# Segment maxima in two levels with an earlier return, and the fourth pass's degree gathers moved to the third pass

## What is computed

```
x += GAT2(GAT1(h))        # two attention layers, 4 heads, self loops
x += sum_e v[src]*s / sum_e s,  s = exp(clip(k[src].q[dst]/sqrt(32)))
x += poincare(h' + attention sum of h'[src])   # one head
x += relu-GCN twice, with norm = w * rsqrt(deg_out[src]*deg_in[dst] + 1e-12)
```

```
e  = leaky_relu(al_s[src] + al_d[dst])
m  = segment_max(e, dst)
ee = exp(e - m[dst]);  s = segment_sum(ee, dst)
out = segment_sum(ee / s[dst] * feat[src], dst)
```

## Time and profile before

| what | value |
| --- | --- |
| median of three runs | 5259.4 us |
| the profiled execution: device time | 5256.77 us |
| its span, first to last instruction | 5255.0 us |
| mean granted TensorE clock | 0.926 of full speed |
| TensorE matmul, busy | 4453.1 us (85%) |
| VectorE, busy | 4208.4 us (80%) |
| ScalarE, busy | 2973.3 us (57%) |
| GpSimd, busy | 3241.2 us (62%) |
| HBM traffic | 209 GB/s mean |

### The profile page before, as it was taken

One profiled execution on the slowest core, in us unless ns is written; L12 is line 12 of the kernel. 1 busy time (PEld: TensorE's weight loads), 2 busy tenths in 40 slices (PEclk: granted clock), 3 DMA queues, 4 the chain that ended last, 5 costly groups with the idle time before them and its releaser, 6 DMA issues. The chain is left out here.

```text
span 5255.0 us, 75793 instructions
## 1 busy us (share of the span) xinstructions
PE 4453.1 (85%) x21191; PEld 3340.7 (64%) x21191; DVE 4208.4 (80%) x12564; ACT 2973.3 (57%) x7552; POOL 3241.2 (62%) x2813
## 2 busy tenths in 40 slices
PE   3999999999958888857888799999956748988887
PEld 2888888888836666635666566666634436765555
DVE  5999999999968888759999478888868878965554
ACT  2999999999914444424444467777745534431111
POOL 3776666666267776447777265555277746647777
PEclk9999999999979999968888899999978878999998
DMA  4888888888734444347777556566457766654443
GB/s 134 300 313 309 311 310 310 308 311 309 287 123 129 128 127 127 95 121 250 256 269 264 174 159 190 184 182 191 157 183 253 254 219 187 204 155 133 151 151 130
DMA packets 645561, 1096.74 MB, mean 209 GB/s; under 512 B 82230, under 2 KB 465654, under 8 KB 645021
## 3 DMA queue, kind: packets, MB, share of 16 engines
q1 hardware_dynamic: 525866, 837.50, 46.5%
q0 software_dynamic: 119168, 253.97, 16.5%
q10 hardware_dynamic: 112, 0.40, 0.0%
HBM read 523.88 MB, written 575.95 MB: 209 GB/s over the span
## 5 line engine op out<-in xcount | busy, mean ns | idle before, releaser
L851 PE MATMUL mm<-w,tt 128*128 128x264 f32 x3136 | 733.6, 387 | 2.6 <-ACT tt L895 2.6
L1399 POOL DMA_INDIRECT got<-F,index x392 | 506.1, 1291 | 281.5 <-PE acc L1557 176.6
L851 PEld LDWEIGHTS mm<-w,tt 128*128 128x128 f32 x3136 | 583.1, 191 | 93.3 <-ACT tt L895 2.8
L1566 ACT ACTIVATE rows<-acc 128x260 f32<-128x260 f32 (+1 forms) x588 | 227.4, 387 | 561.0 <-PE acc L1557 561.0
L1553 PE MATMUL acc<-got,sel 128*128 128x260 f32 (+1 forms) x1176 | 426.1, 449 | 99.6 <-DVE sel L1528 93.2
L817 POOL DMA_INDIRECT place<-PLACE,place_ix x392 | 412.9, 1053 | 119.5 <-issue 119.5
L2698 DVE SCALAR_TENSOR_TENSOR agg<-mask,agg,acc 128x128 f32<-128x128 f32 x784 | 248.0, 344 | 255.7 <-PE acc L2685 141.3
L789 POOL DMA_INDIRECT xd<-in_x_dram,index x196 | 229.5, 1171 | 315.5 <-DMA XD<-xd 284.5
L851 PE MATMUL mm<-wl,tt 128*128 128x264 f32 x1568 | 413.7, 387 | 1.3 <-ACT tt L895 1.3
L1288 PE MATMUL kv<-wkv,ht 128*128 128x512 f32 x784 | 372.7, 598 | 0.1
L1206 POOL DMA_INDIRECT got<-Q,index x196 | 202.0, 1030 | 260.4 <-DVE sc L2284 213.9
(11 more groups left out here) (391 smaller groups left out, 13285.4 us busy)
## 6 DMA issues: line engine op xcount, KB each, us to landing
F<-f1o SPq DMA_DIRECT2D x97, 528.0 KB, 5.9
F<-f2o SPq DMA_DIRECT2D x97, 528.0 KB, 3.2
HL<-ho SPq DMA_DIRECT2D x97, 528.0 KB
xin<-in_x_dram SPq DMA_DIRECT2D x97, 512.0 KB, 5.8
H<-h SPq DMA_DIRECT2D x97, 512.0 KB, 3.4
X<-x3o SPq DMA_DIRECT2D x97, 512.0 KB, 3.4
out_dram<-oo SPq DMA_DIRECT2D x97, 512.0 KB
drow<-DSTF SPq DMA_DIRECT2D x84, 448.0 KB
```

Source lines behind the costliest of these rows:

```text
L851: last = nc.tensor.matmul(mm[PAIR[stage, q]][:, r, 0:F2W], lhs[:, q, 2 * r + k, :], w[:, k, :], start=(k == 0), stop=(k == KB - 1))
L1399: nc.gpsimd.indirect_dma_start(out=buf[:, n % SLOTS, t, :], out_offset=None, in_=table, in_offset=bass.IndirectOffsetOnAxis(ap=index[:, n ...
L1566: nc.scalar.activation(self.rows[:, n % 2, t, :], self.acc[tile % 2][:, 0:self.width], ACT.Copy)\
```

## The change

The maxima are found in two levels. `turn_scores` makes one transpose: head and tile together (28 rows, or 7) become partitions, the 128 edges of a tile the free dimension. `segment_most` scans the 128 edges forward and back, for all tiles at once (`near`), then multiplies the first and last column with an identity (`edges`). `turn_back` makes two matmuls with a matrix of ones, which put each tile's first and last maximum on all partitions (`ends`), and one transpose of `near`. `differences` runs two scans of 8 numbers per head over the tiles of the group (with tables `across_tiles` that say where a target spans a whole tile), adds a penalty where an edge's target is not the neighbouring tile's (`beyond`), and takes the maximum of the three. What is carried to the next group is written by ScalarE behind the exponentials. The tables are made once, at the head of the first pass. `penalties` issues two DMAs per head (8, or 2), each of 7 rows of 128 numbers, in place of one. The turn back stands behind tile 2 in the first and second pass and behind tile 1 in the fourth. The 84 degree gathers of the fourth pass are issued in the third pass, two behind the gathers of each of the first 42 groups.

```
             def turn_scores(self, pe, n):
                 hold(pe, self.done["top"], n + 1, None)
                 hold(pe, self.done["most"], n, None)
-                for t in range(GS):
-                    last = nc.tensor.transpose(self.turned[0:self.h, t * P:(t + 1) * P], self.top[:, t, :], ident[:, :])
-                last.then_inc(self.done["turned"], 1)
+                nc.tensor.transpose(self.turned[0:self.h * GS, 0:P], self.top[:, :, :].rearrange("p h t -> p (h t)"),
+                                    ident[:, :]).then_inc(self.done["turned"], 1)
 
             def segment_most(self, dve, link, n):
-                V, H, s = nc.vector, self.h, n % 2
-                hold(dve, self.pen_in[s], 16 * (n // 2 + 1), None)
+                V, C, s = nc.vector, self.h * GS, n % 2
+                hold(dve, self.pen_in[s], 32 * self.h * (n // 2 + 1), None)
                 hold(dve, self.done["turned"], n + 1, None)
-                hold(dve, self.done["most"], n, None)
+                link(V.tensor_tensor_scan(self.fwd[:, :], self.pen[:, s, 0, :], self.turned[0:C, 0:P], -BIG,
+                                          ALU.add, ALU.max))
                 hold(dve, self.done["back"], n, None)
-                link(V.tensor_tensor_scan(self.fwd[:, :], self.pen[:, s, 0:SE], self.turned[0:H, 0:SE],
-                                          self.bwd[:, 1 - s, SE - 1:SE], ALU.add, ALU.max))
-                V.tensor_tensor_scan(self.bwd[:, s, ::-1], self.pen[:, s, 1:SE + 1][:, ::-1], self.fwd[:, ::-1], -BIG,
-                                     ALU.add, ALU.max).then_inc(self.done["most"], 1)
+                link(V.tensor_tensor_scan(self.near[:, ::-1], self.pen[:, s, 1, ::-1], self.fwd[:, ::-1], -BIG,
+                                          ALU.add, ALU.max))
+                V.tensor_tensor(self.edges[:, :, :], ident[0:C, 0:C].unsqueeze(1).to_broadcast([C, 2, C]),
+                                self.near[:, ::-(P - 1)].unsqueeze(2).to_broadcast([C, 2, C]), ALU.mult)\
+                    .then_inc(self.done["most"], 1)
                 self.make_way(dve)
 
             def turn_back(self, pe, n):
...
                 hold(pe, self.done["most"], n + 1, None)
                 hold(pe, self.done["diff"], n, None)
-                for t in range(GS):
-                    nc.tensor.transpose(self.back[:, t, :], self.bwd[:, s, t * P:(t + 1) * P], ident[0:H, 0:H])
-                nc.tensor.matmul(self.back[:, GS, :], self.bwd[:, 1 - s, SE - 1:SE].to_broadcast([H, P]),
-                                 ident[0:H, 0:H], start=True, stop=False)
-                nc.tensor.matmul(self.back[:, GS, :], self.bwd[:, s, 0:1].to_broadcast([H, P]),
-                                 self.less[:, :], start=False, stop=True).then_inc(self.done["back"], 1)
+                nc.tensor.matmul(self.ends[:, 0, :, 1:GS + 1], self.ones[:, :], self.edges[:, 0, :], start=True, stop=True)
+                nc.tensor.matmul(self.ends[:, 1, :, 0:GS], self.ones[:, :], self.edges[:, 1, :], start=True, stop=True)
+                nc.tensor.transpose(self.back[:, 0:C], self.near[:, :], ident[0:C, 0:C]).then_inc(self.done["back"], 1)
 
+            def differences(self, dve, link, n):
                 V, H, K = nc.vector, self.h, self.kinds
                 hold(dve, self.done["back"], n + 1, None)
+                hold(dve, self.done["past"], n, None)
+                flat = self.over[:, :, :].rearrange("p k x -> p (k x)")
+                ends = self.back[:, 64:64 + 16 * H]
+                V.tensor_tensor_scan(flat[:, 0:8 * H], across_tiles[:, n, 0, 0:8 * H], ends[:, 0:8 * H], -BIG,
+                                     ALU.add, ALU.max)
+                link(V.tensor_tensor_scan(flat[:, 39:39 + 8 * H][:, ::-1], across_tiles[:, n, 1, 0:8 * H][:, ::-1],
+                                          ends[:, 8 * H:16 * H][:, ::-1], -BIG, ALU.add, ALU.max))
+                beside = self.over[:, :, 0:8 * H].rearrange("p k (h t) -> p k h t", h=H)[:, :, :, 0:GS]
+                k = link.go(V.tensor_tensor(self.far[:, :, :, :], beside,
+                                            beyond[:, :, n * GS:(n + 1) * GS].unsqueeze(2).to_broadcast([P, 2, H, GS]),
+                                            ALU.add))
...
+                    r = link.go(V.tensor_tensor(self.ratio(n), before, here, ALU.subtract))
+                link.need(k)
+                k = link.go(V.tensor_tensor(self.peak[:, :, :], self.far[:, 0, :, :], self.far[:, 1, :, :], ALU.max))
...
+                    V.tensor_scalar(self.ratio(n), self.ratio(n), 0.0, None, ALU.min)
+                link.need(k)
+                link(V.tensor_tensor(self.peak[:, :, :], self.peak[:, :, :], self.near_t, ALU.max))
                 V.tensor_tensor(self.weights(n), self.lg[:, :, :, :],
...
             def exponents(self, act, n):
                 hold(act, self.done["diff"], n + 1, None)
                 nc.scalar.activation(self.wt[:, n % 2, :], self.wt[:, n % 2, :], ACT.Exp).then_inc(self.done["wt"], 1)
+                if n + 1 < NS:
+                    nc.scalar.activation(self.ends[:, 0, :, 0], self.reach(0)[:, :, GS], ACT.Copy)\
+                        .then_inc(self.done["past"], 1)
...
             def penalties(self, sp, n):
                 hold(sp, self.done["most"], n - 1, None)
-                sp.dma_start(self.pen[:, n % 2, :], PEN[n * SE:(n + 1) * SE + 1].partition_broadcast(self.h))\
-                    .then_inc(self.pen_in[n % 2], 16)
+                for k in range(2):
+                    for h in range(self.h):
+                        sp.dma_start(self.pen[h * GS:(h + 1) * GS, n % 2, k, :],
+                                     PEN[n * SE + k:(n + 1) * SE + k].rearrange("(t p) -> t p", p=P))\
+                            .then_inc(self.pen_in[n % 2], 16)
```

The place of the turn back in the first pass (in the second, t == 4 becomes t == 2; in the fourth, the call behind the loop moves into it, to t == 1):

```
-                            if within(a) and t == 3:
+                            if within(a) and t == 2:
                                 ph.turn_back(pe, a)
```

The degree gathers on GpSimd, in the third and in the fourth pass:

```
+                    rest = [t for t in range(T) if t % GS >= IN_SECOND]
...
                         ph.gather(pool, at, 1, bound, d["score"], at.n - 1)
+                        gather_degrees(rest[2 * at.n:2 * at.n + 2])
                     unrolled(pool, NG, 0, group)
...
-                        if within(n - SLOTS):
-                            ph.gather_degrees(pool, n - SLOTS, slice(IN_SECOND, None), last_cell)
-                    every(SLOTS, group)
+                    every(0, group)
```

More of the change, by code:

```diff
@@ L1338, in __enter__ @@
                 self.pen_in = self.slots("pen_in", 2)
-                self.done = {k: self.sem(k) for k in ("start", "clean", "warm", "ch", "top", "turned", "most", "back", "diff", "wt",
+                self.done = {k: self.sem(k) for k in ("start", "clean", "warm", "ch", "top", "turned", "most", "back", "past", "diff", "wt",
                                                       "msg", "crow", "acc", "rows", "used", "put")}
@@ L1385, in start_dve @@
             def start_dve(self, dve, link):
+                V = nc.vector
+                V.memset(self.ends[:, 0, :, 0], -BIG)
+                link(V.memset(self.ends[:, 1, :, GS], -BIG))
                 dve.wait_ge(self.done["start"], 1)
-                link(nc.vector.tensor_scalar(self.less[:, :], ident[0:self.h, 0:self.h], -1.0, None, ALU.mult))
-                dve.sem_inc(self.done["start"], 1)
             def gather(self, pool, n, k, bound, free, count):
```

91 lines of the change are left out of this document (66 added, 25 removed).

## The result

The changed kernel takes 5240.9 us (median of 9 runs, 5234.0 to 5246.8) against 5258.4 before (median of 9 runs beside them): ratio 0.9968, 95% interval 0.9957 to 0.9978. It is faster by 17.5 us, where 54 were forecast. The direction is right and the time lies in the range, the size is a third of the forecast. Of all executions in this document, two (5384 us in experiment 1, 5673 us in experiment 3) ran at a lower granted clock; the ratios leave them out, the medians do not.

The account below looks back on a forecast made before the run. TensorE was taken to bound the third pass, loops through several engines the other three. -28 - 15 - 19 + 8 = -54 took the profiled 5256.77 us to 5203; with 2.6 to the median, 5206 us, range 5155 to 5248.

Parts of the forecast that it names:

- the first pass: First pass: a new wait for the maxima replaces the old one; 0.5 gained in 10 groups, 1.3 in 18: -28 us.
- the second pass: Second pass: only the turn back's 0.37 us is on the loop in 20 groups, 0.9 counts in 8: -15 us.
- the saving passes through: Rival, whole kernel: VectorE's saving counts in full, 166 us less, giving 5094; chance 0.06.
- the third pass: Third pass: the degree gathers fit GpSimd's free time, but three pairs delay the start: +8 us, bounds 0 and +15.
- slower rival: Rival, third pass: the degree gathers stall GpSimd, at 4.8 us each giving 5411; chance 0.06.
- SyncE, the tables and GpSimd in the fourth pass cost nothing: SyncE's 7 more DMAs per group and the first-pass tables cost nothing; GpSimd's degree gathers were not on the fourth-pass loop.
- Together 0.35 + 0.65 - 0.25 = 0.75 of about 16.4 a group: Fourth pass: net gain of 0.75 us a group for some 26 groups, -19 us, bounds -7 and -30.
- The start of the sums behind `sel`, 0.35: Fourth pass: sums start behind the score transposes, 4055.43 against `sel` ending at 4055.05, so 0.35 us to gain.
- `th` to `gb`, 0.65: Fourth pass: with the turn back no longer behind the sums, VectorE goes on with `gb` 0.65 us sooner after `th`.
- The turn back in the chain of sums, 0.25: Fourth pass: the turn back between tiles 1 and 2 costs between 0 and its 0.6 us, taken as 0.25.
- lower clock: Rival: less TensorE work lengthens its idle time, every group is of the slow kind, +25 us, giving 5231; chance 0.15.
- the waits eat it: Rival: first-pass turn back always waits for the maxima; first pass gives 0 to -5, second -5, kernel 5241; chance 0.15.

Follow-up runs that it names:

- experiment 1: Changed kernel with the fourth pass's turn back behind the group's seven sums again: 5244.9 us, fourth pass 523.7.
- experiment 3: Changed kernel with 24 transposes of the unit matrix ahead of the fourth pass's score transpose, each group: 5235.1 us, fourth pass 513.9.
- Experiment 11: Changed kernel with first-pass turn back behind the fourth tile's sums and four more scans per group in the second pass: 5233.2 us, passes 765.5 and 716.3.
- experiment 13: Changed kernel with 32 transposes of the unit matrix per group between score transpose and sums in the second pass: 5195.8 us, second pass 669.2.
- experiment 15: Kernel before the change with 28 transposes of the unit matrix per group between score transposes and sums in the second pass: 5243.2 us, second pass 711.5.
- experiment 4: Changed kernel with the degree gathers put back in the fourth pass: 5223.5 us, third pass 815.2, fourth 520.6.
- experiment 10: Changed kernel with the third pass's 84 degree gathers issued behind groups 6 to 47, not 0 to 41: 5224.9 us, third pass 815.7.
- experiment 12: Changed kernel with degree gathers back, TensorE kept busy by 38+8 transposes and late turn back in the fourth pass: 5190.8 us, fourth pass 489.2.
- experiment 8: Kernel before the change with 36 transposes of the unit matrix ahead of each group's score transposes in the fourth pass: 5234.1 us, fourth pass 479.9.
- experiment 5: Changed kernel with degree gathers back and 38 unit-matrix transposes ahead of the scores' and 8 behind in the fourth pass: 5169.6 us, fourth pass 471.4.
- experiment 2: Changed kernel with seven transposes of the scores in place of one in the fourth pass: 5237.6 us, fourth pass 500.0.
- experiment 6: Changed kernel with degree gathers back and seven transposes of the scores in place of one in the fourth pass: 5225.2 us, fourth pass 520.4.

## Why the forecast was right, and where it failed

**Right: the first pass** (-28 forecast, -32 measured). The turn back takes TensorE 0.62 us (forecast 0.6) in place of 0.97, and the steady periods are 24.57 to 25.34 us in place of 25.47 and 26.33: about 1.2 less, where the forecast averaged 1.0. Experiment 11 shows that TensorE's own order, not VectorE's late part, is the loop. The new place of the turn back is no part of the gain: it costs 9 us.

**Right: the second pass** (-15, -16). The parts fit too: the first four periods give 7.7 us, about VectorE's 2.0 each, and the other 23 give 6.4, 0.28 each, near the turn back's 0.35 (the forecast had 8 x 0.9 and 20 x 0.37). That VectorE's saving otherwise lies beside the loop is shown by experiment 11. It holds at this clock only: experiments 13 and 15 show that with TensorE kept at the full level VectorE's saving comes through, 42 us or 1.5 a group of the 2.0 saved. The rival "the saving passes through" had the mechanism and lacked its condition.

**Right in mechanism, a little short: the third pass** (+8, +11). TensorE's waits for rows at the start sum to 26.0 us, and to 18.0 without the degree gathers (experiment 4); experiment 10 shows that the steady part pays nothing. In other kernels with the same third pass it took 832.5 us, with a wait of 7 us in the fifth group; the term should have been 10 to 17. The slower rival's long gathers did not come: the median was 1.00 us, the longest 1.77.

**Right: SyncE, the tables and GpSimd in the fourth pass cost nothing** (experiment 4 for GpSimd; the trace shows no wait for the penalty loads; the first scan starts 24.1 us after its pass with the tables and 24.2 without).

**Wrong: the fourth pass** (-19 forecast, +13 measured), a miss of 32 us; in the profiled execution the whole forecast missed by 31 (-22.7 for -54), in the medians by 37. The step that failed is "Together 0.35 + 0.65 - 0.25 = 0.75 of about 16.4 a group": its last term is too small, and it puts the change in the low level at nothing. The terms as means of 22 groups, before and after:

- The start of the sums behind `sel`, 0.35: from 1.43 to 1.18 us after the start of `sel`, 0.25.
- `th` to `gb`, 0.65: from 0.85 to 0.23, 0.62.
- The turn back in the chain of sums, 0.25: the chain grew by 11.16 - 9.69 = 1.47. Of this 1.10 goes with the turn back's place (experiment 1), where 0.48 is its own price at the full level (experiment 12), twice what I took. The other 0.37 is there without it. At the full level the chain takes 8.57 in the kernel before (experiment 8) and 8.58 with the late turn back (experiment 12), so all but the 0.48 is the low level.

Together 0.25 + 0.62 - 1.47 = -0.60 a group, and the period grew by 0.57.

By experiments 5 and 8 the change is worth -8.5 us in this pass without the low level, and the low level costs 49 in place of 27: +22. By experiments 1 and 12, 8 of the 22 come with the two levels of maxima and 15 with the turn back's early place. Of the miss of 32, 22 is the clock and 10 a smaller gain at the full level: there the first sum starts 1.18 after `sel` before the change too, so that the 0.35 is not there, and the turn back costs the 0.48, against which `th` to `gb` gives 0.73 (0.96 to 0.23), so 0.25 a group is left of the 0.75 (the period gives 15.23 - 14.96 = 0.27). The forecast had the "lower clock" rival, at 0.15 and with 0.9 a group for the groups that were not slow already; it read the low level as two kinds of group, took its fourth-pass rows from a group of the shortest kind, and had no row for a turn back in the low stretch, where it takes TensorE 1.05 us against 0.60 at the full level. Its argument against itself (shorter periods raise the busy share) turned round in this pass: less work, clock 0.78 to 0.75.

The other three passes came to -38 us where -35 were forecast; that the total lies inside the range in spite of the fourth is owed to the range's width. The rival "the waits eat it" names 5241 us, the time measured, and that is luck: it has the first pass give 0 to -5, and it gave -32.

The Trainium skill ("TensorE: Matmul & The Clock Gate", section "HAM oscillation — how this bites in real kernels") has matmul bursts between waits pay for the return from the throttled state in each round and not once. The traces agree: in 27 of 28 groups of the fourth pass the first pairs of sums run at the low level, and 46 transposes in the waits take it away. Its case there waits for DMA; here TensorE waits for VectorE.

Open: why the low stretch lasts longer after the change. The trace shows one transpose in place of seven and a second idle gap of 0.96 us; experiments 2 and 6 undid both and gave 500 and 520, so restoring them is not enough each time. With the turn back behind the sums the first pair at 0.60 comes 4.9 us after the first sum in the median group, against 3.4 before and 5.1 after.

## What to carry to other kernels

When a pass is a loop with idle time on TensorE, don't price an edit at one clock level: read what pairs of matmuls last right behind each idle stretch, and count how long they stay long, over many groups and not in one. Work put into the stretch behind the idle time costs more there (here 1.10 us a group for a turn back that costs 0.48 at the full level). Before optimizing such a loop, run it once with harmless transposes in the idle time: here that told what the clock hid and which engine was the bound behind it. The gathers moved to a pass with room for them were free only behind the pass's start.

## What the runs showed that I had not expected

- Transposes of the unit matrix into unused PSUM, 46 a group, made a pass 49 us shorter (520.6 to 471.4) and raised the granted clock from 0.75 to 0.94; 32 a group in the second pass made it 41 us shorter at clock 0.85 to 0.94.
- 38 such transposes took 4.31 us at the full level, 0.113 each; six of the scores' own took 1.45 at the low one, 0.24 each.
- One kernel's executions (experiment 6) lay between 5199 and 5229 us; the two shortest had the highest granted clock over the whole program, 0.927 and 0.925, the others 0.917 to 0.923. With TensorE kept busy in that pass the range was 5167 to 5173 (experiment 5) and 5189 to 5196 (experiment 12), but in the kernel before 5226 to 5237 (experiment 8), so a narrower range is not shown in general.
